# Moving the multiplication of expert results by their gates from VectorE to ScalarE, with the interleaving of the blocks planned anew

## The reference

```python
probs = jax.nn.softmax(logits, axis=-1)
top_v, top_i = jax.lax.top_k(probs, top_k)          # top_k = 2
gates = jax.nn.softmax(top_v, axis=-1)
comb = jnp.sum(jax.nn.one_hot(top_i, E, dtype=gates.dtype) * gates[..., None], axis=1)
for e in range(E):                                  # E = 8
    y = _swiglu(normed, gate_up_w[e], down_w[e])
    out = out + comb[:, e, None] * y
out = out + _swiglu(normed, shared_gate_up_w, shared_down_w)
```

## Time and profile before

| | |
|---|---|
| median of three runs | 658.55 us |
| span of the profiled execution, first to last instruction | 581.5 us |
| the profiled execution's own time | its span is all that is given of it; the median is 77.05 us above the span |
| PE, DVE, ACT, POOL busy | 500.6, 388.7, 330.0, 332.0 us |
| the 15 multiplications of line 1297 | 18.3 us |
| loads of results (line 515) | 15, of 512 KB each |

### The profile page before, as it was taken

How to read it: one execution, slowest core, us unless ns; L and a number is a source line. 1 busy time by engine, 2 the same in 40 slices (tenths; PEclk the granted TensorE clock), 3 DMA queues, 4 the chain that set the end, 5 groups by cost and what they waited for, 6 DMA issues and landing times.

```text
span 581.5 us, 14497 instructions
## 1 busy us (share of the span) xinstructions
PE 500.6 (86%) x3928; PEld 458.6 (79%) x3928; DVE 388.7 (67%) x1688; ACT 330.0 (57%) x792; POOL 332.0 (57%) x491
## 2 busy tenths in 40 slices
PE   2588999989999989999977499996899999799781
PEld 1466999979899989998974369794889989799780
DVE  5558864732558989879887958999785624222574
ACT  3367556565467777667753357673655546555430
POOL 2273766875565675356674405664566765565542
PEclk9989999999999999999977569997999999999996
DMA  6944858766886554766412254431668767676993
GB/s 184 316 112 167 261 188 237 243 233 239 284 260 218 190 187 173 258 226 205 155 47 59 69 195 176 160 112 54 209 224 257 248 221 246 228 262 237 322 320 124
DMA packets 88012, 117.82 MB, mean 203 GB/s; under 512 B 11848, under 2 KB 60880, under 8 KB 87936
## 3 DMA queue, kind: packets, MB, share of 16 engines
q1 hardware_dynamic: 76208, 96.75, 49.8%
q0 software_dynamic: 9312, 19.16, 9.5%
q10 hardware_dynamic: 2416, 0.99, 0.7%
HBM read 26.57 MB, written 26.19 MB: 91 GB/s over the span
## 4 chain that ended last, share of the span: by engine, by line
PE 52%; SPq 15%; ACT 9%; DMA 7%; issue 7%; DVE 5%; POOL 3%; ACTq 1%; POOLq 0%; DVEq 0%
PE ps_y L730 12%; PE ps_g L716 11%; PE ps_u L721 6%; SPq L441 6%; PE ps_h L721 5%; DMA xin<-rows 5%; SPq L484 4%; SPq L479 3%; PE ps_x L711 2%; PE w L630 2%; SPq L499 2%; POOL rows L1572 2%; ACT zz L849 2%; PE w L660 2%; PE w L616 2%
## 5 line engine op out<-in xcount | busy, mean ns | idle before, releaser
L1589 POOL DMA_INDIRECT results<-raw_gu,idx x163 | 164.6, 1010 | 144.8 <-ACT raw_gu L929 103.1
L1572 POOL DMA_INDIRECT rows<-zz,s_idx x128 | 126.0, 984 | 66.9 <-issue 28.3
L730 PE MATMUL ps_y<-dn_t,raw_gu 128*128 x978 | 139.2, 279 | 5.7 <-ACT raw_gu L929 5.0
L716 PE MATMUL ps_g<-x_t,raw_dn 128*128 128x128 f32 x978 | 137.5, 277 | 0.0
L730 PEld LDWEIGHTS ps_y<-dn_t,raw_gu 128*128 128x128 f32 x978 | 123.4, 193 | 9.3 <-issue 8.5
L716 PEld LDWEIGHTS ps_g<-x_t,raw_dn 128*128 128x128 f32 x978 | 122.8, 192 | 3.6 <-issue 3.5
L929 ACT COPY raw_gu<-ps_y 128x128 f32<-128x128 f32 x163 | 42.9, 263 | 103.5 <-PE ps_y L730 101.8
L923 ACT ACTIVATE sil<-ps_g 128x384 f32<-128x384 f32 x163 | 80.1, 491 | 22.0 <-PE ps_g L716 20.8
L920 ACT ACTIVATE x_t<-ps_x,bf_c,gf_c 128x128 f32<-128x128 f32 x163 | 75.3, 462 | 19.6 <-PE ps_x L711 19.4
L1397 DVE TENSOR_TENSOR raw_gu<-sil,ps_u 128x384 f32<-128x384 f32 x82 | 44.9, 548 | 54.2 <-PE ps_u L721 47.2
L1397 DVE TENSOR_TENSOR raw_gu<-sil,ps_h 128x384 f32<-128x384 f32 x81 | 44.5, 550 | 50.8 <-PE ps_h L721 35.9
(11 more groups left out here) (172 smaller groups left out, 729.0 us busy)
## 6 DMA issues: line engine op xcount, KB each, us to landing
raw_dn<-gu_t SPq DMA_DIRECT2D x163, 384.0 KB
xin<-rows SPq DMA_DIRECT2D x163, 64.5 KB
yg<-results SPq DMA_DIRECT2D x15, 512.0 KB, 5.1
results<-raw_gu,idx POOLq DMA_INDIRECT x163
rows<-pads SPq DMA_DIRECT2D x40, 64.5 KB
rows<-pads SPq DMA_DIRECT2D x5, 451.5 KB
rows<-zz,s_idx POOLq DMA_INDIRECT x128, 2.4
out<-xres SPq DMA_DIRECT2D x7, 256.0 KB, 3.3
```

What stands on the lines that cost most here:

```text
L716: t = pe.matmul(ps_g[k][:, c, :], ws[:, k4, c * P:(c + 1) * P], x_t[:, k, :], start=True, stop=True)
L730: t = pe.matmul(ps_y[:, 0, :], h_t[:, k4, c * P:(c + 1) * P], dn[:, bass.ds(off + c * D, D)], start=(c == 0), stop=(c == FC - 1))
L1572: pool.indirect_dma_start(xs, bass.IndirectOffsetOnAxis(s_idx[n][:, c, k:k + 1], 0), zz[n][:, k, c, :], None).then_inc(scat[n], 16)
L1589: pool.indirect_dma_start(yt, bass.IndirectOffsetOnAxis(idx[:, ky:ky + 1], 0), yb[:, ky, :], None).then_inc(yst[ky], 16)
```

## The change

ACT multiplies each loaded result by its gate in place, one tile and one of the two copies at a time: 8 instructions `activation(Copy)` of 128 columns with the gate as the scale, of one value for each partition. ACT waits for the load itself. DVE waits for the eight pieces (a new semaphore `ym`) and does the two additions alone.

The combine of step p stands in ACT's order behind the exponentials of the turn before and ahead of the scores of this one (for steps 0 and 3 ahead of their normalisation; for the combines of layer 1 at the end, in `for J in range(...)`). `WEAVE` is new for all five engines.

```diff
         N_TOP = 2 * TB * (KTOP // 8)
         N_SCAT = 2 * TB * 16
-        N_CB = 3
+        N_CB = 2
+        N_YM = 2 * TB
...
+            def weighed(C, n, tile):
+
+                act.wait_ge(yld[n], (C - n) * 8 + 16)
+                act.wait_ge(gts, C // STEPS + 1)
+                for c in range(2):
+                    for k in range(TB):
+                        act.activation(yg[n][:, k, c, :], yg[n][:, k, c, :], ACT.Copy,
+                                       scale=gates[:, c, tile + k:tile + k + 1]).then_inc(ym, 1)
+                        turn()
...
                 a, A, J, p = f[:4]
                 if a in ALONE:
+                    weighed(a, a % 2, a * TB)
                     norm_x(a, chain_alone[a])
...
+                if p is not None:
+                    weighed(p, p % 2, p * TB)
                 if a is not None:
                     scores(a)
...
             gates_of_layer(1)
+            for J in range(PHASE[-1].lo):
+                weighed(STEPS + J, J % 2, J * TB)
             turn.rest()
...
             def combine(C, n, tile):
 
-                dve.wait_ge(yld[n], (C - n) * 8 + 16)
-                of = gates[:, :, tile:tile + TB].rearrange("p c (t o) -> p t c o", o=1).broadcast_to([P, TB, 2, D])
-                dve.tensor_tensor(yg[n][:], yg[n][:], of, ALU.mult).then_inc(cb, 1)
-                turn()
+                dve.wait_ge(ym, C * N_YM + N_YM)
                 xr = xres[:, tile:tile + TB, :]
                 for c in range(2):
-                    dve.wait_ge(cb, C * N_CB + 2 * N_CB + c + 1)
+                    if c:
+                        dve.wait_ge(cb, C * N_CB + 2 * N_CB + c)
                     dve.tensor_tensor(xr, xr, yg[n][:, :, c, :], ALU.add).then_inc(cb, 1)
                     turn()
```

More of the change, by code:

```diff
@@ L114 @@
     "sp": """
-        8 7 3 8 2 2 13 8 24 12 4 45 9 13 12 1 48 9 7 z1 14 22 38 4 4 z1 1 z1 5 z1 3 z6""",
+        7 2 6 12 z2 16 1 33 5 6 50 1 9 22 z2 61 1 7 6 4 62 2 7 1 1 z1 3 z1 1 z6""",
     "pe": """
-        z5 2 2 z1 1 z1 3 z2 1 z1 2 4 2 z2 8 4 3 z2 2 5 4 z1 1 5 2 6 4 z1 6 5 4 z2 98 3 z1 3 6 8 3 z1 5 3 2 3 12 5 z1 5 5 2 5 7 4 4 12 1 22 3 z1 3 z1
-        3 3 8 z1 3 z2 6 7 z1 3 2 5 4 2 z1 1 z2 1 z7 1 2 1 z1 3 7 z1 6 1 2 10 5 1 z3 4 9 z1 5 z1 1 5 z3 7 z1 2 3 11 3 3 6 z1 21 5 3 4 z1 22""",
+        z4 1 1 5 1 z4 1 z2 4 5 3 z2 2 9 4 z2 2 3 2 z1 1 3 5 5 z1 3 5 8 2 6 z1 93 3 z1 3 2 14 4 z1 3 3 3 4 8 5 3 3 5 4 2 10 2 2 11 1 28 2 z1 3 1
@@ L119 @@
+        6 3 4 1 z3 4 9 z1 4 z1 5 3 5 z4 1 z6 1 z2 2 1 3 7 z1 1 3 4 5 10 3 1 z2 2 7 z1 5 1 5 2 z3 7 z1 5 2 16 2 2 5 z1 20 4 1 4 z1 4""",
     "act": """
-        z12 1 1 z2 1 z1 2 3 z5 1 1 z4 1 6 3 1 z3 1 4 2 2 z4 5 2 z1 3 z3 9 4 2 11 5 56 2 z2 2 3 z1 3 7 z3 3 3 z4 1 4 2 z1 8 z2 1 2 3 1 z4 6 z1 4 4 z1
-        2 z1 2 4 3 z1 1 z2 21 z3 3 2 z1 2 2 z1 5 1 z6 2 z1 2 1 1 4 2 z3 5 2 3 3 z4 1 z2 1 z3 1 1 z15 1 z1 1 1 z1 2 z1 1 z2 8 z1 4 8 z8 1 2 z2 3 2 1
-        z2 4 z1 5 3 z6 3 z3 3 8 z4 2 3 3 15 1 z1 1 4 z1 3 40 15 1""",
+        z12 2 4 z5 2 z5 1 3 z2 1 2 z1 3 1 7 z4 3 1 z2 1 z1 2 2 3 1 z1 1 1 z1 6 4 6 8 4 48 1 z6 11 z2 1 2 3 z9 1 10 1 z2 2 3 z13 3 z1 4 4 z1 1 2
@@ L123 @@
+        2 3 3 z3 2 2 1 4 3 z1 1 z1 5 1 z1 3 2 4 z1 7 z1 1 z5 12 z3 3 1 z9 2 2 4 3 z8 1 1 1 z2 6 z3 2 z7 3 z1 5 4 z2 1 z4 1 z5 1 z22 1 z2 2 z1 2
+        z1 1 z4 2 z3 2 z1 3 z1 3 6 z1 2 1 z2 2 z2 3 1 z3 3 z1 1 z1 6 1 4 1 z8 1 2 6 2 8 z3 3 2 z1 17 z3 3 3 1 9 5 98 z6 2 2 z6 3 8 z15 8 z3 1
+        z10 1 2 z8""",
     "dve": """
-        z153 1 z1 1 z4 1 z20 1 z11 1 z4 1 z5 1 z2 1 z9 1 z16 2 z7 2 z2 1 z9 2 z2 1 z13 1 z3 1 1 z1 1 z2 8 1 3 3 1 z2 1 z5 1 z4 1 z1 1 1 z3 1 z6 1 z5
-        2 z13 1 z9 1 z2 1 z2 1 z7 1 z5 1 1 z10 2 z25 1 z1 1 z2 1 z10 2 z4 1 z7 1 z15 1 z10 1 z6 2 z9 1 1 z4 1 z9 2 z1 1 z13 2 z5 1 z12 1 z10 1 z2 2
@@ L126 @@
-        z20 1 z10 1 z7 2 z4 1 z29 1 z101 1 z3 1 z17 1 z1 1 z3 1 z6 1 z2 1 z10 1 z3 1 z14 1 z17 1 z13 1 z7 1 z15 1 z10 1 z2 1 z46 1 z24 2 z15 1 z5 1
-        z8 1 z24 1 z4 2 z19 1 z1 1 z9 2 z1 2 z30 1 2 z10 9 z5 5 z2 2 z2 9 4 1 3 1 1 z1 1 z3 3 z2 1 1 z2 3 z6""",
+        z137 1 z3 1 z2 1 z21 1 z6 1 z4 1 z14 1 z4 1 z12 1 z15 1 z5 1 z5 1 z5 2 z1 1 z8 1 z1 1 z6 1 z10 1 z4 1 1 z2 16 z1 1 z3 1 z2 1 z6 3 z1 1
+        z13 1 1 z19 2 z8 1 z3 1 z6 1 z5 1 z2 1 z2 1 z7 1 z20 1 z1 1 z4 1 z8 1 z6 1 z3 1 z11 1 z8 1 z13 2 z9 3 z1 1 z3 1 z4 1 z4 2 z1 1 z18 1
@@ L128 @@
+        z15 1 z12 1 z4 1 z9 1 z3 1 z12 1 z7 1 z2 1 z5 1 z19 1 z101 1 z6 1 z20 2 z1 1 z9 1 z6 1 z3 1 z9 1 z2 1 z19 1 z11 1 z10 1 z1 1 z12 1 z20
+        1 z42 1 z8 1 z2 1 z10 1 z6 1 z5 1 z11 1 z6 1 z25 1 z5 1 z11 1 z7 1 z1 1 z16 3 z25 1 z14 1 z1 1 z5 2 z2 33 z1 2 z1 2 z3 4 z6""",
     "pool": """
-        z21 2 1 z1 1 z3 4 z2 3 z1 1 2 z1 5 1 2 2 1 1 3 1 2 z2 1 1 3 3 2 5 16 4 13 4 5 5 z1 5 1 1 2 2 z1 3 z2 2 5 31 z2 3 z1 5 4 z1 2 1 z1 5 1 z3 3
-        z10 8 1 7 z1 2 1 1 1 2 2 z3 6 z4 3 z2 1 3 z1 5 5 1 4 2 2 2 z2 3 7 z3 10 7 1 10 3 3 10 40""",
+        z18 1 z1 1 z2 1 1 2 z2 2 z1 2 z1 3 z3 3 3 z1 1 1 z2 5 1 1 1 3 z1 2 1 z1 1 2 2 5 5 z1 2 5 9 z1 1 z1 4 5 3 1 1 z1 2 3 44 4 4 2 z1 6 z1 1
@@ L131 @@
+        1 12 z3 4 z2 5 z1 1 z8 6 2 2 z1 1 2 z1 1 z1 10 z2 1 1 z1 2 z1 2 6 z2 4 3 z2 1 1 5 z1 3 1 6 1 2 2 1 3 1 z1 1 3 5 1 6 4""",
 }
@@ L332, in macaron @@
             sem(n) for n in ("tl", "tl_e", "bl", "ended", "tab", "gts", "run0", "padded"))
-        cb = sem("cb")
+        cb, ym = sem("cb"), sem("ym")
         yld = [sem(f"yld{n}") for n in range(2)]
@@ L356, in macaron @@
                    (y_ps, 8), (y_sb, 6), (shh, 1), (xr_done, 1), (prT_sb, 1), (pr_done, TB), (ex_done, TB),
-                   (nm_done, 1), (o_ps, 1), (o_sb, 1), (v_sb, 1), (x2_done, TB), (cb, 2 * 3)]
+                   (nm_done, 1), (o_ps, 1), (o_sb, 1), (v_sb, 1), (x2_done, TB), (cb, 2 * 2)]
         ctx.enter_context(nc.allow_low_precision(reason="rows' numbers are whole and below 2**24, exact in float32"))
```

## The result

The changed kernel takes 711.36 us (median of 4 runs, 709.25 to 715.97), the kernel before 659.51 us (4 runs, 658.46 to 661.50): ratio 1.083, 95% interval 1.076 to 1.091. The forecast was 665.5 us with a range up to 671. The sign was right; the size was off by 46 us, and the time lies outside the range.

What follows compares the result with a forecast made beforehand. Blocks filling PE, the attention's chain across engines and the tail of loads and combines were taken to bound the kernel in turn. Six terms summed to +7.0 us on 658.55, giving 665.5 us; range 652.5 to 671, own range 662 to 670.

Steps and rivals of the forecast that it cites:

- I make the sum on the span and leave the 77.05 alone: Whole kernel: terms summed on the profiled span of 581.5 us; the 77.05 us up to the median of 658.55 left unchanged.
- The rest of the new order: Start, weights, fills, scatters: same instructions at other places, PE positions meet again at 84y; 0, with 3 us either way.
- other losses by the new order: Leftover case beside the named rivals: the new order loses time in other ways; chance 0.02.
- The six terms: Combine 0 +4.1, combine 3 +1.2, combines 1, 2, 4, 5 +1.2, VectorE late -2.4, block 85's load -0.5, tail +3.4.
- combine 0: Load issued later, ScalarE waits some 3 us, PE transposes block 39 later: +4.1 us, bounds 0 and +5.1.
- combine 3: Load now behind 68g and its reading, ScalarE's copies later, PE loses part: +1.2 us, bounds 0 and +2.6.
- VectorE's relief: Combines 5 and 6, where VectorE is late: 1.2 us comes off for each, -2.4 us, bounds 0 and -3.7.
- DVE's relief wins: Rival: eight multiplications leave VectorE's order between 150 and 360 us, starved stretches shrink; 652.5 us, chance 0.20.
- One sign of being wrong: PE between blocks 84 and 85: an idle stretch shorter by more than 3 us would show the forecast wrong.
- The tail's +3.4: From 535 us: longer load periods, last results loaded behind the output of combine 14; +3.4 us, bounds 0 and +6.4.
- Moved, nothing gained: Rival: PE's losses at combines 0 and 3 are slack lost anyway; +1.0, 659.5 us, chance 0.23.
- dearer pieces: Rival: pieces 0.388 us apart, 4.4 us more at combines 0 and 3 and in the tail; 670 us, chance 0.12.

Runs made afterwards that it cites:

- e1: The kernel before, unchanged, run and traced again: 649.0 us, span 647.2 us.
- e2: The changed kernel with its new order of all engines, but VectorE multiplying as before: 693.53 us, ratio 1.060 to the kernel before.
- e17: The new order with VectorE multiplying, run once more with more runs: 695.63 us, ratio 1.069 to the kernel before.
- e12: The kernel before with 48 row scatters of layer 0 one block part later in POOL's order: 658.82 us, ratio 1.012.
- e13: The kernel before with 45 row scatters of layer 0 one block part earlier in POOL's order: 658.45 us, ratio 1.014.
- e3: ScalarE multiplies in eight pieces, in the old order of all engines: 671.26 us, ratio 1.028 to the kernel before.
- e16: The changed kernel unchanged, once more with more runs, on another chip than its earlier single execution: 705.05 us, ratio 1.082 to the kernel before.
- e7: The kernel before with VectorE's multiplication cut to 1 of 128 columns and nothing put in its place: 656.78 us, ratio 1.003.
- e4: The changed kernel, unchanged, traced again in one execution: 695.92 us, 6.8% over the kernel before.
- e15: Old order; ScalarE multiplies in the tail alone (combines 8 to 14), VectorE in combines 0 to 7: 657.00 us, ratio 1.010 to the kernel before.
- e8: The kernel before plus eight extra ScalarE pieces in each of combines 0 to 7 that VectorE doesn't wait for: 662.09 us, ratio 1.012.
- e10: The kernel before with the new order for POOL alone: 686.58 us, ratio 1.049.

## Why the prediction was wrong

**The execution that the sum was made on.** "I make the sum on the span and leave the 77.05 alone" is a step that failed, though no term of the sum hangs on it. The 77 us were not a constant beside the span. By e1 some 65 of them were inside it: 11 in one wait ahead of the first block, most of the rest in the stretches where routing or attention runs beside blocks, which a new order changes. A span 12% under the median was the sign that the trace was of an execution unlike the timed ones, and I passed over it. In the short execution PE was busy 38.2 of 40 us at 140 to 180, in e1 35.7: how near each stretch was to waiting can't be read from a trace in which nearly everything ran on time. Whether the trace of e1 would have shown what the order costs is another question; nothing here says so.

**"The rest of the new order": 0, with 3 us either way.** This is the step that made the error. e2 and e17 put it at 39 to 45 us (6.0% and 6.9%). I took PE's positions, which differ by a block or so and meet again, as a bound for the time. e12 and e13 show that a shift of one place on one engine's queue is worth 8 to 9 us, so no such bound was to be had. And "issues the same instructions" passed over four more table loads on ScalarE, at most 5 us. "I can't price it from rows of before" was right; the 3 us were a guess in a bound's clothes, and the range was built on them. The chance of 0.02 for "other losses by the new order" stood where the result fell.

**The pieces.** Price: eight pieces were to take 2.46 us to their end; they take 2.45 in e3, and one lasts 390 to 392 ns:

```profile
184.35 2.45 ACT L844 ACTIVATE yg<-yg,gates 128x128 f32<-128x128 f32 x8 [0.33 <-DMA yg<-results]
```

Price and work were right: ScalarE is busy for 334.1 us in e2 and 366.9 in the changed kernel, 32.8 more, where 35.5 were forecast. The six terms sum to +7.0 us in the new order; e16 over e17 gives 8 us. But that the sum comes so near is luck, as the single terms don't hold.

At combine 0 the piece waited 1.95 us where some 3 were foretold, and the additions behind it 4.1 us; yet PE turns block 39 (its transposition) 7.0 us behind block 37, where e1 has 6.2 and the trace of before 6.0: 1 us instead of 4.1. At combine 3 block 69 comes 10.5 us behind block 65, where e1 has 10.4: 0.1 instead of 1.2. VectorE's relief, -2.4, measured nothing or less (e7, in the old order), so the term should have been 0, and the rival "DVE's relief wins" falls with it. One sign of being wrong did come: from block 84's up product to block 85 PE has 30.7 us instead of 37.6 in e1 (its idle time in there falls from 16.2 to 14.1). But e2 has 31.0 there with VectorE multiplying, so it is the order's doing. What made up the pieces' 8 us isn't shown.

The tail's +3.4: from the load of combine 8 to the end are 48.5 us in e1 (647.2 - 598.7) and 51.9 in the changed kernel (710.9 - 659.0). That this is +3.4 is luck too: two more traces of the changed kernel have 50.0 (e4) and 52.5 (e16), the new order with VectorE multiplying has 50.5 (e2), and in the old order the pieces cost 4.6 (e15, 53.1) and 6.7 (e3, 55.2). The last results are indeed loaded behind the output of combine 14 now (SP's lines of the changed kernel), but e2 has SP's load behind the last addition too, at 687.51:

```profile
658.96 0.39 SPq L517 DMA_DIRECT2D yg<-results  x1
...
693.73 0.44 SPq L517 DMA_DIRECT2D yg<-results  x1
696.49 6.07 SPq L523 DMA_DIRECT2D out<-xres  x2
703.43 0.37 SPq L407 DMA_DIRECT2D raw_gu<-results  x1
```

"Moved, nothing gained" (+1.0) fits the 8 us badly, and "dearer pieces" falls by the row of eight: at 0.388 us apart it would last 3.1 us and not 2.45. The rule of the Trainium skill (ScalarE: Activation LUTs, Rules for kernel authors), multiply on VectorE, gave 677 with all latencies laid bare, 18.6 us over before; in the old order e3 lost 18 to 20. The agreement is of the sum only: e8 and e15 put some 8 us of it on ScalarE's time in the attention stretch and some 6 on the tail, and not on 15 equal latencies.

**What stays open.** Why a shifted order costs what it does. The costs of the parts don't add (3.2 + 5.3 against 6.0; 0.2 + 4.9 + 4.1 against 6.0), which speaks for a rhythm between block work and routing that is lost once, whatever breaks it; the equal loss at block 9 fits that. No run shows the mechanism, so it is known which step of the prediction failed and by how much, but not why an order costs what it does. Which single move of the new order on PE, ACT or DVE costs wasn't tried.

## What to carry to other kernels

Compare the span of a profiled execution with the timed median before anything else: where they are far apart, the trace may be of an unlike execution, and sums made on it need a second trace. When a change moves both a piece of work and a hand-planned order of five queues, test the two apart: here two short variants showed that 6 to 7 of the 8% came from the order and not from the edit that the change was named after. VectorE, idle a third of the time and more, gave nothing for being relieved here. And an order found by planning may be a narrow optimum, so price a new one as a risk of several per cent and not as zero.

## What the hardware showed

In the longer executions a consumer often starts 1 to 4 us after the recorded end of the matrix products that it waits for, with its engine idle and nothing else in the timeline. From e10:

```profile
94.22 0.46 ACT L921 ACTIVATE x_t<-ps_x,bf_c,gf_c 128x128 f32<-128x128 f32 x1
...
95.07 0.60 PE L610 MATMUL w<-ident,zz 128*128 128x128 f32 x4
96.70 0.69 DVE L1198 SCALAR_TENSOR_TENSOR xres<-w,xres 128x512 f32<-128x512 f32 x1 [1.33 <-PE w L680]
98.13 0.78 ACT L876 ACTIVATE nz_t<-w,bf_c,gf_c 128x512 f32<-128x512 f32 x1 [3.44 <-remote]
```

The four transpositions end at 95.67 by the record, and ScalarE, idle since 94.68, takes them up at 98.13. I added up such late starts of ScalarE and VectorE at the four steps of a block (over 0.3 us behind the recorded end of what they read, worked out from the records). They come to under 1 us in the trace of before, 77 in e1, 125 in e2 and 144 in the changed kernel: the slower kernels mostly have more of them, though not strictly (66 in e13). They lie for the most part where routing or attention runs beside blocks; from block 130 on they are 13 of the 77 in e1 and 2 of the 125 in e2.

The consumers are not what is late. The trace also records when PE raises the semaphore that a consumer waits for: 98.10 us for the transpositions above, 46.63 us for the product whose record ends at 35.59 in e1 (the wait of 12.28 us). In e1 this is so for 43 of the 44 late starts on ScalarE, each within 0.1 us of PE's signal. So the delay is on PE's side, between the modelled end of its products and its signal. What holds PE up there isn't on record.

The granted clock explains less than half of the difference between the two traces of the kernel before: its mean is 0.951 in the trace of before and 0.913 in e1. PE was at its lower level of 1.2 GHz in 115 us of e1 after the first 20 us, in 59 of the trace of before, worked out from the records of the clock; at half speed the 56 us more are worth at most 28 of the 66 us between them, and e10 has PE late at 95 to 98 us, in a stretch at full clock.
